# A Macaron block on one Trainium2 core: group products from rounded halves, row transfers issued later, row numbers read back later

## What is computed

```python
x = x + 0.5 * ffn(layernorm(x))       # 32 experts
x = x + attention(layernorm(x))       # 16 heads of 32, cumulative sums
x = x + 0.5 * ffn(layernorm(x))       # the same experts again

# ffn, per sequence: softmax of the gate's logits over the 1024 rows;
# every expert takes its 8 strongest rows, merges them with their weights,
# runs one hidden layer (512 -> 2048 -> 512) on the merged row,
# and adds its output, times each weight, back to those 8 rows
# attention: q = exp(q), k = exp(k);  out = q.(cumsum k v) / q.(cumsum k)
```

## Time and profile before

| what | value |
|---|---|
| median of 3 runs | 2288.2 us (2282.41 to 6017.0) |
| the profiled execution | 2283.05 us |
| its span in the profile | 2281.3 us |
| busy in the span | PE 86%, PEld 51%, ACT 34%, DVE 32%, POOL 27% |
| first pass over the experts, about 145 to 912 us | PE without gaps, DMA share about 1.0 |
| attention, about 912 to 1650 us | PE busy seven to nine tenths in the page's slices, DMA six or seven tenths |
| second pass, from about 1650 us | DMA 9 tenths or more to the end, PE six or seven |

### The profile page before, as it was taken

One profiled execution on the slowest core, in us unless ns is written; L12 is line 12 of the kernel. 1 busy time (PEld: TensorE's weight loads), 2 busy tenths in 40 slices (PEclk: granted clock), 3 DMA queues, 4 the chain that ended last, 5 costly groups with the idle time before them and its releaser, 6 DMA issues.

```text
span 2281.3 us, 43539 instructions
## 1 busy us (share of the span) xinstructions
PE 1962.4 (86%) x18440; PEld 1161.6 (51%) x18440; DVE 728.5 (32%) x1235; ACT 779.3 (34%) x1413; POOL 622.9 (27%) x756
## 2 busy tenths in 40 slices
PE   5789999999999999889999999999776566656667
PEld 4546666666666666666777776777521111111111
DVE  6731111111111111367777677677410000000011
ACT  6831111121111111357777777677510000000000
POOL 7610000000000000267777777777412000000002
PEclk9999999999999999999999999999897867787777
DMA  9999999999999999776776676676499999999997
GB/s 366 357 398 404 418 401 428 430 426 422 427 418 429 418 423 415 219 261 212 250 262 224 229 249 214 198 258 209 184 406 425 427 399 428 428 428 428 428 427 332
DMA packets 133202, 804.49 MB, mean 353 GB/s; under 512 B 31240, under 2 KB 31368, under 8 KB 91792
## 3 DMA queue, kind: packets, MB, share of 16 engines
q1 hardware_dynamic: 116880, 713.29, 79.0%
q10 hardware_dynamic: 9216, 50.34, 5.3%
q0 software_dynamic: 6912, 38.07, 4.3%
HBM read 678.24 MB, written 136.95 MB: 357 GB/s over the span
## 4 chain that ended last, share of the span: by engine, by line
PE 59%; DMA 24%; ACT 5%; POOL 5%; issue 4%; SPq 1%; DVE 1%; POOLq 0%; DVEq 0%; ACTq 0%
PE ps L349 54%; DMA big<-in_L_ffn_w 22%; PE ps L353 3%; SPq L18 1%; DMA last_scratch<-idx 1%; ACT big L635 1%; POOL big L1599 1%; POOL s L1602 1%; ACT big L620 1%; PE ps L824 1%; POOL big L1572 1%; ACT big L625 1%; DMA row_scratch<-idx 1%; PE ps L512 0%; ACT big L1391 0%
## 5 line engine op out<-in xcount | busy, mean ns | idle before, releaser
L349 PE MATMUL ps<-big 128*32 128x512 f32 (+5 forms) x13568 | 946.7, 412 | 229.9 <-DMA big<-in_L_ffn_w 179.9
L349 PEld LDWEIGHTS ps<-big 128*32 128x32 f32 (+2 forms) x13568 | 374.1, 126 | 727.4 <-issue 383.6
L357 DVE TENSOR_TENSOR big<-ps,big 128x128 f32<-128x128 f32 (+4 forms) x277 | 266.7, 966 | 697.9 <-PE ps L824 511.6
L349 PE MATMUL ps<-wth,xth 128*128 128x512 f32 x768 | 311.8, 406 | 1.5 <-DVE xtl L357 1.5
L349 PE MATMUL ps<-wtl,xth 128*128 128x512 f32 x768 | 299.6, 390 | 0.0
L349 PE MATMUL ps<-wth,xtl 128*128 128x512 f32 x768 | 299.3, 390 | 0.0
L872 ACT COPY big<-ps 128x512 f32<-128x512 f32 x64 | 37.5, 586 | 644.1 <-PE ps L349 623.3
L1544 POOL TENSOR_SCALAR big<-big 128x1 f32<-128x1 f32 x8 | 1.5, 188 | 827.6 <-ACT ps L1351 827.2
L1024 DVE TENSOR_SCALAR big<-ps,big 128x512 f32<-128x512 f32 x64 | 48.1, 751 | 533.7 <-PE ps L349 533.7
L1015 ACT ACTIVATE big<-ps,big 128x512 f32<-128x512 f32 x128 | 88.2, 689 | 371.8 <-PE ps L349 356.1
L349 PE MATMUL ps<-wo,s 128*128 128x512 f32 x768 | 210.0, 408 | 3.0 <-ACT s L1436 1.4
(11 more groups left out here) (140 smaller groups left out, 1761.8 us busy)
## 6 DMA issues: line engine op xcount, KB each, us to landing
big<-in_L_ffn_w SPq DMA_DIRECT2D x254, 2048.0 KB, 35.9
p_weight_x_scratch<-big ACTq DMA_DIRECT2D x64, 768.0 KB, 11.2
big<-p_weight_x_scratch SPq DMA_DIRECT2D x64, 768.0 KB, 5.7
xt_scratch<-big SPq DMA_DIRECT2D x16, 1024.0 KB, 8.6
big<-xt_scratch SPq DMA_DIRECT2D x16, 1024.0 KB, 16.2
x_weight_scratch<-big SPq DMA_DIRECT2D x64, 256.0 KB, 3.2
out_x<-big SPq DMA_DIRECT2D x64, 256.0 KB, 4.0
big<-in_L_attn_x SPq DMA_DIRECT2D x15, 1024.0 KB, 11.3
```

Of the source, the lines that this page charges most:

```text
L349: return nc.tensor.matmul(o, l, r, start=start, stop=stop, skip_group_check=True)
L357: return nc.vector.tensor_tensor(o, p, q, op)
```

## The change

The products of batches 2 to 7 (`rows_pe`) become three products of rounded halves each, 12 matmuls where 4 stood. For that ACT makes a rounded copy `OSH[b]` of the experts' outputs and DVE the rest `OSL[b]` (both at step n = 8b-11), and DVE makes a rounded copy and a rest of the transposed weights (`GWP`). POOL issues the gathers and scatters at the end of the step, behind L1599, L1602 and the scale, where they stood ahead of L1599. SP reads the row numbers back at expert 8 where it did so at expert 6.

```diff
+        OSL = [halves(f"osl{b}", os_at + 512 * b, 512) for b in range(8)]
+        OSH = [None, None] + [halves(f"osh{b}", os_at + 512 * (b - 1), 512) for b in range(2, 8)]
+        GWP = [halves(f"gwp{i}", os_at + 256 * i, 256) for i in range(2)]
...
                 if p == 0 and e == 6:
                     rows_sp(sp)
+                if p == 0 and e == 8:
+                    rows_read_sp(sp)
...
                     if turn(n - 1, 2):
-                        pe.wait_ge(s_gwt, GW0 + turn(n - 1, 2) - TILED + 1)
+                        pe.wait_ge(s_gwt, gwts(turn(n - 1, 2)))
...
+                if n >= 0 and turn(n, 1):
+                    rows_outer_act(act, turn(n, 1))
...
+                if n >= 0 and turn(n, 1):
+                    rows_outer_dve(dve, turn(n, 1))
                 if turn(n, 2):
                     rows_weights_dve(dve, turn(n, 2))
...
                     nc.gpsimd.tensor_tensor(ATL, AT, ATH.bitcast(F), ALU.subtract).then_inc(s_atl, 1)
-                for i in range(2):
-                    if turn(n, i):
-                        rows_gather_pool(pool, turn(n, i), i)
-                for i in range(2):
-                    if turn(n, 5 + i):
-                        rows_scatter_pool(pool, turn(n, 5 + i), i)
                 m = n + 2
...
                 if 8 * TILED <= n + 3 < NT:
                     pool.wait_ge(s_kl, n + 3)
                     scale_pool(n + 3)
+                for i in range(2):
+                    if turn(n, i):
+                        rows_gather_pool(pool, turn(n, i), i)
+                for i in range(2):
+                    if turn(n, 5 + i):
+                        rows_scatter_pool(pool, turn(n, 5 + i), i)
...
+        def rows_outer_act(act, b):
+            act.wait_ge(d_os[b // 4], 16 * 16)
+            act.wait_ge(s_gc, GC0 + 2 * (b - TILED))
+            act.wait_ge(s_c, 8)
+            nc.scalar.copy(OSH[b], OS[b]).then_inc(s_osh, 1)
+
+        def rows_outer_dve(dve, b):
+            dve.wait_ge(s_osh, OH0 + b - 1)
+            tt(OSL[b], OS[b], OSH[b].bitcast(F), ALU.subtract).then_inc(s_osl, 1)
...
                 sp.dma_start(idxd[h], IDX1[:, 8 * h:8 * h + 8]).then_inc(d_row, 16)
+
+        def rows_read_sp(sp):
             sp.wait_ge(d_row, RW0 + 32)
...
-            if b > 1:
+            if b == 1:
+                nc.vector.tensor_copy(at(m_at + 2048, 256), ps[:, 4, 0:256]).then_inc(s_gwt, 1)
+            else:
                 dve.wait_ge(s_c, 8)
-            nc.vector.tensor_copy(at(os_at if b > 1 else m_at + 2048, 256), ps[:, 4, 0:256]).then_inc(s_gwt, 1)
+                nc.vector.tensor_copy(GWP[0], ps[:, 4, 0:256]).then_inc(s_gwt, 1)
+                dve.wait_ge(s_gwt, gwts(b) - 1)
+                tt(GWP[1], ps[:, 4, 0:256], GWP[0].bitcast(F), ALU.subtract).then_inc(s_gwt, 1)
...
+                pe.wait_ge(s_osl, OL0 + b - 1)
+                for v, (w, o) in enumerate(((0, OSH[b]), (0, OSL[b]), (1, OSH[b]))):
+                    for u in range(4):
+                        R_ = slice(32 * u, 32 * u + 32)
+                        t = mm(ps[:, 4 + u, :], GWP[w][R_, 128 * i:128 * i + 128], o[R_, :], v == 0, v == 2)
```

More of the change, by code:

```diff
@@ L147, in macaron_block @@
         G = [at(w_at + 2 * SLOT - 64 + XP * i, XP) for i in range(2)]
-        GWT = [[at(p + 128 * i, 128) for i in range(2)] for p in (m_at + 2048, os_at)]
+        GWT = [at(m_at + 2048 + 128 * i, 128) for i in range(2)]
+        OSL = [halves(f"osl{b}", os_at + 512 * b, 512) for b in range(8)]
+        OSH = [None, None] + [halves(f"osh{b}", os_at + 512 * (b - 1), 512) for b in range(2, 8)]
+        GWP = [halves(f"gwp{i}", os_at + 256 * i, 256) for i in range(2)]
         MTK = [at(m_at + 2048 + 256 * b, 256).rearrange("p (c e) -> p c e", c=8) for b in range(8)]
@@ L267, in macaron_block @@
         s_gwt, GW0 = s_nm4, NG
+        s_osh, OH0 = s_nma, NG + NG // 2
+        s_osl, OL0 = s_ocl, 2
         s_gc, GC0 = s_lg4, NG
@@ L1627, in rank_pool, with gwts @@
                     nc.gpsimd.memset(ROW0[h][32 * q:32 * q + 32, :], float(S * (4 * h + q) - 1)).then_inc(s_rank, 1)
+        def gwts(b):
+            return GW0 + 2 * b - 1
+        def rows_outer_act(act, b):
[6 more added lines that the diff above has]
+            tt(OSL[b], OS[b], OSH[b].bitcast(F), ALU.subtract).then_inc(s_osl, 1)
         def rows_pool(pool):
@@ L1689, in rows_weights_dve @@
             dve.wait_ge(s_gc, GC0 + 2 * (b - TILED))
-            if b > 1:
+            if b == 1:
+                nc.vector.tensor_copy(at(m_at + 2048, 256), ps[:, 4, 0:256]).then_inc(s_gwt, 1)
+            else:
                 dve.wait_ge(s_c, 8)
-            nc.vector.tensor_copy(at(os_at if b > 1 else m_at + 2048, 256), ps[:, 4, 0:256]).then_inc(s_gwt, 1)
+                nc.vector.tensor_copy(GWP[0], ps[:, 4, 0:256]).then_inc(s_gwt, 1)
+                dve.wait_ge(s_gwt, gwts(b) - 1)
+                tt(GWP[1], ps[:, 4, 0:256], GWP[0].bitcast(F), ALU.subtract).then_inc(s_gwt, 1)
         def rows_pe(pe, b, i):
-            pe.wait_ge(s_gwt, GW0 + b - TILED + 1)
+            pe.wait_ge(s_gwt, gwts(b))
             pe.wait_ge(d_os[b // 4], 16 * 16)
             pe.wait_ge(s_ga, GA0 + 2 * (b - TILED) + i)
-            for u in range(4):
-                R_ = slice(32 * u, 32 * u + 32)
-                t = mm(ps[:, 4 + u, :], GWT[b > 1][i][R_, :], OS[b][R_, :], True, True)
+            if b == 1:
+                for u in range(4):
+                    R_ = slice(32 * u, 32 * u + 32)
+                    t = mm(ps[:, 4 + u, :], GWT[i][R_, :], OS[b][R_, :], True, True)
+            else:
+                pe.wait_ge(s_osl, OL0 + b - 1)
+                for v, (w, o) in enumerate(((0, OSH[b]), (0, OSL[b]), (1, OSH[b]))):
+                    for u in range(4):
+                        R_ = slice(32 * u, 32 * u + 32)
+                        t = mm(ps[:, 4 + u, :], GWP[w][R_, 128 * i:128 * i + 128], o[R_, :], v == 0, v == 2)
             t.then_inc(s_gc, 1)
```

## The result

| | median of the runs | ratio to before, 95% interval | profiled execution | its span |
|---|---|---|---|---|
| before | 2286.91 us (6 runs beside the changed kernel) | | 2283.05 us | 2281.3 us |
| changed | 2332.07 us (6 runs) | 1.0195 [1.0178, 1.0212] | 2335.98 us | 2333.9 us |

The change costs 45 us; 2323 was forecast, within 2290 to 2348. One of the six executions before took 6017.0 us; without it their median is 2285.63. The two profiled executions lie on opposite sides of their medians, so the spans differ by more, 52.6 us, and 2.8 us of that come from the gate stage, in which the code is the same and which differs from run to run. In the changed kernel the lines are numbered a little higher: matmuls are L354, the mask L362, the gather L1692, the scatter L1701, ACT's rounding L1647, DVE's rounded copy of the weights L1720.

What follows compares the result with a forecast made beforehand. PE's order was taken to bound the attention, where nearly all the change lies; terms of +26.5 +8.3 +10 -4.8 -2 +3.6 -1 -1 = 39.6 us on 2283.05 gave 2322.7, called 2323, range 2290 to 2348.

Steps and rivals of the forecast that it cites:

- Part 1: Attention, weights' transposes: PE waits for late second gathers, 5.3 us in each of batches 3 to 7 (26.5), 8.3 in batch 2.
- the second rival: Attention's late gathers: flight of 4.4 us, waits 11.4 us in all, clock does not fall; 2289 us, 12%.
- Part 2: Attention, behind each new PE wait: granted clock falls to 0.50, some 1.7 us lost, six times: 10 us more.
- Part 3: Attention, POOL: late second scatter no longer delays k's low half, 0.8 us less in six batches: 4.8 us less.
- Part 4: Attention, products on PE: halves' matmuls run beside each other, 0.96 us for 1.14, 12 times: 2 us less.
- The third rival: Attention, products on PE: halves run one after another, 3.0 us, 23 us more over 12 times; 2348 us, 8%.
- Part 5: Attention, steps 8b-11: rounded copy on ACT adds 0.6 us, six times, 3.6 us more; DVE's work and PE's waits add nothing.
- Part 6: Attention's start, batch 1: ACT's scale comes earlier but gathers leave later; 1 us less, between 4.8 less and 2 more.
- Part 7: First pass over the experts: reading row numbers at expert 8 removes the pause at expert 6, 1 us less.
- the ends 2298 and 2342: The forecast case's own range for the whole kernel, from waits of 3.2 to 5.8 us and clock loss 0 to 18.
- the first two rivals: Attention's late gathers: still in time, 2278 us, 6%; or a 4.4 us flight without a clock fall, 2289 us, 12%.

Runs made afterwards that it cites:

- the last run above: Changed kernel with gathers, first scatters and batch 1's second scatter back ahead of the scale, rounding a step later, second scatters late from batch 2: 2277.48 us.

## Why the prediction was right, and where its terms were off

**Part 1, the gathers: right, by its own steps.** The issue of batch 5's second gather moved from 8.2 to 13.3 us behind the start of step 29, 5.1 us against 4.9 forecast; the hardware queue shared the engines with it as in the earlier trace rows; PE waited 4.99 us against 5.3. The other four waits are 5.08, 5.32, 4.05 and 4.66 us, 24.1 with it against 26.5, and batch 2's 8.64 against 8.3. Putting the gathers back removed them; moving them alone brought them all. The sentence that each batch's first gather sets nothing holds in the changed kernel, where it leads the second by a whole step; it does not hold when the second is back at its old place and follows after 6 us.

The rule quoted there from the Trainium skill (DMA: Bandwidth & Descriptors, the rules for kernel authors: issue early, wait late) is what these runs show, 40 us of it. The Trainium skill's figure for one DMA (DMA: Bandwidth & Descriptors, Anatomy of one DMA), an estimate of 4.4 us for this gather, is not what they show: 6.2 us in a pause of the other queue, 8.0 beside it. With it fell the second rival, a shorter flight without a fall of the clock.

**Part 2, the clock: right.** Each wait was followed by a stretch at 0.50, and keeping PE busy through it took 1.9 us off a step of batches 3 to 7, against 1.7. At batch 2 no run held the clock, so its 1.7 is not shown apart.

**Part 3, the scatters: the term was mis-sized.** The forecast took 0.8 us back in each of six batches for the second scatter and put the first one's move at nothing, because that had cost nothing at its old place. With both late the steps 3 mod 8 got shorter by 0.86 us in four batches and by 0.3 and 0.4 in the other two, but the steps 2 mod 8 longer by 0.73 in those four (shorter by 0.24 in the two). Together -1.6 in place of -4.8. The runs separate the two: in those with both late, wherever gathers and rounding stand, steps 26 and 27 are 10.5 and 9.7 us, and in those with the second alone late 9.7 and 10.0 (before 9.8 and 10.55). So the second alone gains 0.6 a batch, in the last run above 3.7 in all against before, and the first's late place takes more than half of that again. The sentence that the later landing harms nobody counted SP's loads only: once the gathers are back, POOL's next gather waits for it, 2.63 and 1.42 us.

**Part 4, the products of halves: right.** One half's products are now these three rows, where before stood 1.14 us for eight records.

```profile
1252.37 0.50 PE L354 MATMUL ps<-osh,gwp 32*128 32x512 f32 x4
1252.71 0.40 PE L354 MATMUL ps<-osl,gwp 32*128 32x512 f32 x4
1252.94 0.40 PE L354 MATMUL ps<-osh,gwp 32*128 32x512 f32 x4
```

Four products with 32 rows each lie beside each other, a round every 0.23 to 0.34 us, and 12 matmuls end after 0.97 us; 0.96 was worked out. The step gains 0.16. The third rival (one after another) asked for 3.0 us and is out. The Trainium skill's rule of four row groups at once (TensorE: Matmul & The Clock Gate, Part 3), which names no rounded halves, holds for them here.

**Part 5, the rounding: right but for one place.** The steps 13, 21, 29, 37 and 45 grew by 0.37 to 0.53 us (0.6 forecast). Batch 2's grew by 4.67. The step that failed is the count of waits: I named PE's new waits and found that they pass, but not ACT's, and so did not ask when PE makes batch 0's last product and what stands behind the rounding on ACT. With the rounding a step later, or without it, step 5 is 11.5, so 4.3 of the 4.67 us are the rounding's.

**Part 6, the start: wrong in sign.** I took 1 us less, between 4.8 less and 2 more; it is 5.1 us more. The sentence "the gathers leave some 5 us later and the weights wait for them soon after" was in the forecast without being carried through as in part 1: PE waits 7.25 us where it had 2.35 at the scale. Against the first mask the two gathers leave 6.7 us later, and the second's packets are in 9.8 us after its issue, where it was 7.1. With the gathers back, step 0 is 15.42 again.

**Part 7, the row numbers: right.** The chain of waits has no DMA in the first pass at expert 6 any more, and the 27.30 us of the earlier trace rows are 26.15 from one expert's products to the next (25.68 + 0.47):

```profile
292.07 0.47 PE ps L831 x4
292.55 23.95 PE ps L354 x136
316.49 0.47 PE ps L831 x4
316.96 25.68 PE ps L354 x140
342.65 0.47 PE ps L831 x4
```

**The sum.** Forecast 39.6 us on the profiled execution, measured 52.6: 13 more. The three terms that were off make 13.4 (4.1 in step 5, 6.1 at the start, 3.2 from the scatters), the others lie 3.4 under their forecasts together, and 2.8 stand in the gate stage, which the change doesn't touch. Of the ranges, the ends 2298 and 2342 don't follow from the bounds named beside them, which give 2300 and 2334 with the other terms as they are, and 2290 lies above the times of the first two rivals (2278 and 2289). The measured 2332 lies near the upper end of 2300 to 2334, because the three terms that were off all erred to the same side.

## What to carry to other kernels

A DMA's issue may be moved behind other work only as far as its data lay ready ahead of the reader; that slack is read from issue, last packet and first use in one timeline, at every place where the loop's pattern differs, the first turns above all. A moved transfer also moves whoever waits for its landing: a scatter issued late holds back the next gather. A new instruction on a full engine brings its waits with it, and everything queued behind it pays for the longest of them.

## What was not expected of the hardware

The flight of the second gather, from issue to last packet, depended on the place, at the same 144 packets and 1.07 MB: 5.6 to 7.0 us at the old place in batches 2 to 7 (6.2 in batch 5), 7.1 to 8.2 at the new one beside tile loads in batches 3 to 7, 9.3 at batch 2 and, with the first one just in front of it, 9.8 at the start. And the granted clock was at 0.50 behind each of PE's waits of 3.75 to 9.64 us that the attention had in these runs, while behind waits of about 2 us both levels occurred. In the run with only the first gather late, behind a wait of 2.00 us (to 1302.87, the row shown there) and behind one of 2.09 us (to 1133.70), in windows:

```profile
1303.20:1306.50 3.30, 3.30 (x22) 2.52 (x15) 2.23 (x5) 1.37 (x3) 0.33 (x1) 0.50 0.80 311
1133.80:1137.10 3.30, 3.06 (x30) 2.37 (x31) 2.23 (x5) 2.13 (x4) 0.47 (x1) 1.00 0.73 296
```

The first is at 0.50, the second at 1.00; what decides between them is open.
